# Unused TensorE products up to the searches, scatters between gathers, and part of the final addition on TensorE in a routed mixture-of-experts block

## The reference

```python
x = x + einsum('oc,bchw->bohw', W(V), layernorm_over_channels(x))   # W: product of 32 reflections
t = tokens(x)                                                       # 4096 x 128
s = softmax(layernorm(t) @ W_router + b_router)                     # 4096 x 32
G, idx = top_k(s.T, 128)                       # for each of 32 experts its 128 best tokens
up  = silu(layernorm(t)[idx] @ W_up[group] + b_up)                  # 128 x 341, 8 groups of 4 experts
out = G[..., None] * (up @ W_down[expert] + b_down)                 # 128 x 128
y = zeros(4096, 128).at[idx].add(out)          # a token can be chosen by several experts
return images(t + y)
```

## Time and profile before

| | us |
|---|---|
| median of 3 runs (lowest to highest) | 196.4 (196.19 to 196.7) |
| profiled execution, its own time | 196.68 |
| its span in the trace | 194.9 |
| TensorE busy / share of the span | 139.9 / 72% |
| VectorE busy | 108.9 / 56% |
| GpSimd busy | 107.1 / 55% |
| ScalarE busy | 76.1 / 39% |
| chain of waits: TensorE's share | 53% |

### The profile page before, as it was taken

How to read it: one execution, slowest core, us unless ns; L and a number is a source line. 1 busy time by engine, 2 the same in 40 slices (tenths; PEclk the granted TensorE clock), 3 DMA queues, 4 the chain that set the end, 5 groups by cost and what they waited for, 6 DMA issues and landing times.

```text
span 194.9 us, 2467 instructions
## 1 busy us (share of the span) xinstructions
PE 139.9 (72%) x694; PEld 87.6 (45%) x697; DVE 108.9 (56%) x433; ACT 76.1 (39%) x266; POOL 107.1 (55%) x120
## 2 busy tenths in 40 slices
PE   0999965413215347754299997999974999999990
PEld 0557954301104224334134763777652344444690
DVE  2454998984676692110435448458399069945500
ACT  3166899536895675100234252335400000000161
POOL 2028478997560277774356377878768878600000
PEclk9999999955555555557579999999997599999997
DMA  4999999999867062222112223334343333399666
GB/s 96 300 335 309 293 294 208 249 403 285 221 185 217 17 265 70 64 62 60 31 36 50 50 54 42 31 27 40 27 42 28 27 32 39 28 290 344 240 212 222
DMA packets 31982, 28.39 MB, mean 146 GB/s; under 512 B 6784, under 2 KB 25680, under 8 KB 31840
## 3 DMA queue, kind: packets, MB, share of 16 engines
q1 hardware_dynamic: 25777, 22.74, 39.8%
q0 software_dynamic: 5328, 4.41, 15.3%
q10 hardware_dynamic: 864, 1.08, 1.7%
HBM read 17.61 MB, written 10.62 MB: 145 GB/s over the span
## 4 chain that ended last, share of the span: by engine, by line
PE 53%; DVE 14%; POOL 12%; another core or an unknown queue 7%; issue 6%; ACT 3%; DMA 2%; SPq 0%; POOLq 0%; DVEq 0%
PE PZ L1216 9%; PE PT L1178 7%; PE PM L1178 6%; PE PZ L1194 5%; PE PT L1216 4%; PE PM L1216 4%; POOL rs L493 4%; PE PM L1194 3%; POOL rs L486 3%; PE PT L1017 3%; DVE wdn L956 2%; POOL act L499 2%; PE PZ L1221 2%; PE PT L1164 2%
## 5 line engine op out<-in xcount | busy, mean ns | idle before, releaser
L532 POOL DMA_INDIRECT acc<-X,idx x26 | 40.8, 1567 | 12.2 <-issue 8.2
L523 POOL DMA_INDIRECT xg<-token_rows,idx x32 | 30.4, 951 | 21.0 <-issue 9.6
L956 DVE TENSOR_SCALAR_CACHE_REDUCE wdn<-wide,slot_token 128x1024 bf16<-128x1024 f16 x24 | 29.9, 1273 | 7.0 <-PE PZ L1216 7.0
L944 DVE TENSOR_SCALAR_CACHE_REDUCE junk<-PZ,k 128x128 f16<-128x128 f32 x24 | 8.3, 348 | 25.1 <-remote 13.2
L666 ACT ACTIVATE X<-PZ 128x512 f32<-128x512 f32 x4 | 2.4, 598 | 45.1 <-PE PZ L1221 45.1
L1065 PE MATMUL PZ<-stage_w,X 128*128 128x192 f32 x64 | 14.7, 382 | 6.9 <-DVE act L788 6.5
L1194 PE MATMUL PZ<-wdn,act 128*128 128x128 f32 x132 | 18.7, 290 | 1.0 <-DVE X L991 1.0
L1194 PEld LDWEIGHTS PZ<-wdn,act 128*128 128x128 f32 x132 | 17.3, 204 | 2.1 <-DVE X L991 1.4
L1178 PE MATMUL PM<-xgT,wup 128*128 128x512 f32 (+3 forms) x26 | 15.0, 667 | 3.6 <-issue 2.5
L659 ACT ACTIVATE act<-PT,bup 128x512 f32<-128x512 f32 (+3 forms) x14 | 9.0, 641 | 21.4 <-PE PT L1178 14.5
L1178 PE MATMUL PT<-xgT,wup 128*128 128x512 f32 (+3 forms) x28 | 16.4, 672 | 0.9 <-ACT xgT L650 0.9
(11 more groups left out here) (180 smaller groups left out, 280.2 us busy)
## 6 DMA issues: line engine op xcount, KB each, us to landing
X<-in_x SPq DMA_DIRECT2D x8, 256.0 KB, 5.3
acc<-zero SPq DMA_DIRECT2D x4, 512.0 KB, 6.7
acc<-x SPq DMA_DIRECT2D x8, 256.0 KB, 5.9
token_rows<-xf SPq DMA_DIRECT2D x8, 256.0 KB, 2.3
x<-acc SPq DMA_DIRECT2D x8, 256.0 KB, 5.8
out<-X SPq DMA_DIRECT2D x3, 512.0 KB, 3.6
wup<-in_L_ffn_W_up SPq DMA_DIRECT2D x1, 1364.0 KB, 7.8
wdn<-in_L_ffn_W_down SPq DMA_DIRECT2D x1, 1280.0 KB
```

Source lines behind the costliest of these rows:

```text
L523: nc.gpsimd.indirect_dma_start(out=xg[:, e, :], out_offset=None, in_=rows[:, :], in_offset=bass.IndirectOffsetOnAxis(ap=idx[:, e:e + 1], a ...
L532: nc.gpsimd.indirect_dma_start(out=acc[i][:, :], out_offset=bass.IndirectOffsetOnAxis(ap=idx[:, e:e + 1], axis=0), in_=eo[:, e, :], in_off ...
L956: nc.vector.tensor_scalar(hot(k)[:, r], columns[:, r], slot_token[:, k:k + 1], None, ALU.is_equal, ALU.add, accum_out=found_in[:, k * HOT_ ...
```

## The change

It has three parts. First, `keep_warm(n, bank)` issues n products of a 128 x 128 float16 identity with 512 columns of constants into a PSUM bank that nobody reads then; 65 of them are put into TensorE's queue, three in each pass of the mixing loop from g = 5 on, and groups of 1 to 12 between the steps of the searches and the first 16 finds. Their results are not used. Three waits come with them: for all transposed inputs and the constants at g = 5, and for all mixed chunks to be used before the first group of the searches. Second, GpSimd issues 14 gathers (`AHEAD`) instead of 32 before its first scatter; the other 18 gathers follow in six rounds of one scatter and three gathers, and then the 20 scatters that are left. Third, for the first three chunks (`DIRECT`) VectorE doesn't add the accumulators; TensorE adds `y1` and then `y0` to the bank itself.

```diff
-AHEAD = E
+AHEAD = 14
+PER_SCATTER = 3
 EARLY = 4
+DIRECT = 3
...
-            e = 0
+            e, ahead = 0, AHEAD
+            while ahead < E:
+                scatter(e)
+                for _ in range(PER_SCATTER):
+                    gather(ahead)
+                    ahead += 1
+                e += 1
             while e < SCATTERED:
...
-            for g in range(CH):
+            for g in range(DIRECT, CH):
                 v.wait_ge(s_y1[g], 16)
...
+            def keep_warm(n, bank):
+                for _ in range(n):
+                    mm(bank, ident16, kh16[:, 0:512], start=True, stop=True)
+
             pe.wait_ge(s_wst, 1)
             for g in range(CH + KEYS_LAG):
+                if g == XAHEAD + 1:
+                    pe.wait_ge(s_xts, CH)
+                    pe.wait_ge(s_const16, 32)
+                if g > XAHEAD:
+                    keep_warm(3, PT[:, 1, :])
...
             ins.then_inc(s_guess, 1)
+            pe.wait_ge(s_zfree, CH)
+            pe.wait_ge(s_x1, TILES)
+            keep_warm(5, PZ[:, 3, :])
             pe.wait_ge(s_cnta, 1)
             mm(PM[:, 0, 0:1], same_expert_m2, cnt_a[:, 0:1], start=True, stop=True).then_inc(s_sum, 1)
+            keep_warm(4, PZ[:, 3, :])
             pe.wait_ge(s_top8, BLOCKS)
...
+            keep_warm(12, PZ[:, 3, :])
             pe.wait_ge(s_thr, 1)
...
+            keep_warm(1, PZ[:, 3, :])
             pe.wait_ge(s_missed, 1)
...
+            keep_warm(3, PZ[:, 3, :])
             pe.wait_ge(s_flag, 1)
...
             ins.then_inc(s_cum, 1)
+            keep_warm(1, PZ[:, 3, :])
             pe.wait_ge(s_tot, 1)
...
+            keep_warm(4, PM[:, 0, :])
             for e in range(FIRST_FINDS):
                 find(e)
+                if e % 4 == 3:
+                    keep_warm(2, PM[:, 0, :])
...
+            for g in range(DIRECT):
+                pe.wait_ge(s_y1[g], 16)
+                for u in range(TPC):
+                    mm(out_bank(g)[:, u * P:(u + 1) * P], y1[:, g * TPC + u, :], ident, start=False, stop=False)
             for g in range(CH):
-                pe.wait_ge(s_ys, g + 1)
+                if g < DIRECT:
+                    pe.wait_ge(s_y0[g], 16)
+                else:
+                    pe.wait_ge(s_ys, g - DIRECT + 1)
```

## The result

The changed kernel takes 207.24 us (205.36 to 208.51, five runs), against 196.4 us (195.6 to 197.72, five runs) for the kernel before beside it: a ratio of 1.052, with an interval of 1.047 to 1.057. It is slower by 5.2%, where 186.9 us was forecast and 198.3 us was the upper bound. The profiled execution took 207.28 us, with a span of 205.4 us against 194.9 us before: 10.5 us more.

What follows compares the result with a forecast made beforehand. TensorE was taken to set the end from about 97 us, with about 10 us lost to late results before. Span 194.9 - 12.2 + 2.7 = 185.4, plus 1.8 around it, less 0.28: 186.9 us; range 184.0 to 198.3.

Steps and rivals of the forecast that it cites:

- the late results: TensorE's results used about 4 to 9 us late from 79 to 97 us; the forecast took this delay as gone.
- 12.2 us gain of the sum: At unit 8: its gathered rows there at 121.1 us, against its transpose at 133.31 before.
- The late results stay as they are: Rival: expert 0 ready only at 97.2 us, nothing won, additions paid; 199.1 us, or 197.6; chance 0.18.
- its own rule: The late-results rival decides when expert 0 is later than 95.4 us (12.2 won less 2.7 paid).
- They last as long as GpSimd issues without a pause: Rival: GpSimd stops at 85.6 us, expert 0 comes at 91.9; 192.9 us; late in part has chance 0.20.
- Unused products: Mixing loop and searches: hidden at the high clock; from 1.5 us gained to 3.2 + 2 lost.
- Nothing gained and nothing lost up to the first gather: Mixing loop and searches: unused products leave the first gather at 68.4 us.
- the high clock gives back: Searches: half of the 16 selection products' 1.89 us, prefix products and finds likewise; put at 1.5 us.
- the page that the prediction weighed: Skill page: transposes do not count as clock activity; true matmuls would hold the clock; not used in the sum.
- One scatter and three gathers in turn: GpSimd after 14 gathers: six rounds of about 5.6 us, gather 31 at 118.3, last scatter at 158.4 us.
- The rival by which scatters and gathers hold each other up: Interleaved rounds: a microsecond or more lost per round, 192.9 us; chance 0.12 together with clock not held.
- TensorE adds three chunks: Final adds: 12 more float32 transposes cost 2.7 us, paid in full because TensorE ends the kernel.

Runs made afterwards that it cites:

- second set: Kernel before (196.80 us, late results), changed kernel (1.047) and the change with DIRECT = 0 (1.043), all run on one chip.
- third set: Kernel before (196.77 us, late results) beside products alone (0.997), order alone (0.992), pause every four gathers (0.988) and changed kernel (1.022).

## Why the prediction was wrong

**The failed step** is the one that prices the late results: "With the clock high at 74 us I take the delay as gone." It fails twice. Its premise doesn't hold: the clock falls at 71 us in spite of the products. And its inference doesn't hold: the second lateness of the changed kernel begins with the clock at its high level (108.47 us; it is high from 95.0 to 118.9), and the kernel with pauses, in a late set, has none with the clock low until 86.2 us. The low clock and the late results stood in the same rows and had been taken for cause and effect, and the rows of the kernel before held a sign against it: two activations 1.2 and 1.0 us late at 120 us, at the high clock. The whole 12.2 us gain of the sum hung on this sentence; in its place unit 8 came 8.0 us later.

**The rival that had the mechanism** was "The late results stay as they are", and it was sized at 199.1 us. It too falls short by 8 us. It priced the delay as something at a fixed place. By its own rule (expert 0 at 95.4 us) the change should about have broken even with scatter 0 at 95.52 us. GpSimd did keep that pace: gather 31 starts at 128.60, so its rows are there by about 131.4. But the new unbroken row brought the delay a second time, TensorE lost 10.5 us on the kernel before between 105 and 141 us, and transposed these rows at 141.33. The rival "They last as long as GpSimd issues without a pause" had the better law: in the changed kernel the first lateness ends at 87.77 us, about when the fourteenth gather lands (85.52 + 2.8), and in the kernel before it ends behind the pause that starts at 90.64, though 6 us behind it. It holds for rows with gathers in them alone: in the kernel before the scatters from 121.26 to 145 us follow each other in 0.3 to 0.65 us, and no activation between 122 and 139 us is more than 0.1 us late. Its price (192.9 us) was wrong because it followed that law only up to the first scatter and not into the rounds behind it.

**What is shown and what is argued.** That the late results are a matter of GpSimd's row of indirect DMAs is shown for a wait before every fourth gather, which removes them (one kernel, one trace in a late set), and is supported by the places where they come in the three orders. That the condition has to do with this row is supported too, as the events go missing from 70 us on. Whether the recording of events plays a part is not tested. That the second lateness comes with the new order and without the products is shown by the kernel with the order alone (one trace). What in the chip holds the results back is not. Nor is it settled why products and order cost +4.3% together (second set) when each alone measured 0.997 and 0.992 (third set): the changed kernel itself moved from 207.3 to 201.9 us between these sets while the kernel before did not move. Gaps of this size in a delay whose trigger isn't known can't be assigned to a part. Whether a softer pause would do in a late set, and whether the changed kernel with pauses would win there, stays open too: those kernels ran only where nothing was late.

**Unused products.** Nothing gained and nothing lost up to the first gather was nearly right: it starts at 69.25 us against 68.38. Over all traces it starts at 68.7 to 70.8 us with the products and at 68.0 to 68.7 without them and their waits, so about 1 us is lost; the kernel with the three waits but no products has it at 69.07, so part of that may be theirs. The selection products take 1.07 us instead of 1.89, so that the high clock gives back 0.8 us there, about as forecast. Missed was that the clock falls again at 71 us, right behind them. As to the page that the prediction weighed (the Trainium skill, TensorE: Matmul & The Clock Gate, Part 4: PE-mode transpose), true matmuls did bring the clock up between 50 and 71 us, but the stretch from 74 to 88 us held transposes, products and gaps mixed, so that no run separates the two kinds.

**One scatter and three gathers in turn.** The arithmetic held: six rounds of 5.7 us each (5.61 forecast, 5.67 by the forecast's own terms), each time within 2.5 us where nothing was late. The rival by which scatters and gathers hold each other up is refuted. But the gain of 12.2 us at unit 8 compared it with a TensorE that had lost those 12 us to the late results. Against a kernel without them it is worth nothing (0.2%, inside the interval).

**TensorE adds three chunks.** Right: 2.7 us forecast, 2.7 measured in the rows and 2.3 in the medians. Without late results half of it hides behind the read-back.

**No version is better throughout.** The kernel with the pause every four gathers measured 0.988 where results are late, and loses 6.6% where they are not. The order alone measured 0.992 in the one and loses nothing that shows in the other. The intervals of the two overlap, and both gains are near the noise.

## What to carry to other kernels

If a consumer starts several microseconds after the modelled end of its producer, and no engine is named as releaser, that is a delay with an unknown cause; see whether the trace has lost events there, and don't price a change as if it removed it, and ask whether the change makes more of what stood beside it (here unbroken rows of gathers, and of gathers and scatters in turn). Two things that stand in the same rows, such as a low clock and late results, want one experiment each before one is called the cause of the other. Compare kernels only beside their own run of the kernel before: here the condition of the set is worth 12 us, three times the effect of the change where nothing is late.

## What the runs showed of the hardware

The same kernel takes 184 to 185 us in three sets and 197 us in two, and one chip showed both. The difference is made of TensorE's results coming late, by up to 2.8 to 8.6 us in each of eight traces, while GpSimd issues gathers (0.95 us each, 0.3 us apart), or gathers and scatters in turn, in an unbroken row; an unbroken row of scatters alone (1.55 us each) brought none. It comes with the granted clock at either of its two levels. The Trainium skill says, in Perfetto Trace Analysis, Tensor Engine Instruction (MATMUL, LD_WEIGHTS), that a matmul's recorded end is an estimate and that its semaphore follows the acknowledged write to PSUM; the traces agree that recorded ends can be 8 us before the use, and none shows what the write waited for. A wait for the rows' landing before every fourth gather, 1.9 us each, was enough to leave 0.5 us of it at most. In the same condition the traces hold 369 to 564 semaphore events from 70 to 150 us, where the others hold 996 to 1087; why is not known.
